# Picking expert 0's rows by f32r products of high and low parts instead of fp32 products

## The reference

```
h = tokens(x)                                  # patches @ W.T + b, a class token, positions
h = h + attn(layernorm(h))                     # causal sums, rank 64 factors, no softmax
xf = layernorm(h)                              # 1184 x 256
gates = softmax(xf @ w_router + b_router)      # 8 experts
topv, topi = top_k(gates, 2)
pos  = place of each choice in its expert's queue, in row order; keep = pos < cap   # cap = 185
buf[e, pos] = xf[row]                          # 8 experts x 185 rows x 256
out = gelu(buf @ w1 + b1) @ w2 + b2            # 256 -> 1024 -> 256 for each expert
h = h + sum over the two choices of weight * out[e, pos] / sum of kept weights
```

## Time and profile before

| | |
|---|---|
| median of 3 runs | 184.07 us (183.93 to 184.51) |
| the profiled execution | 182.03 us, of which its span is 180.2 us |
| PE busy | 160.3 us (89%) |
| DVE busy | 69.3 us (38%) |
| ACT busy | 62.5 us (35%) |
| POOL busy | 38.5 us (21%) |
[...]

### The profile page before, as it was taken

How to read it: one execution, slowest core, us unless ns; L and a number is a source line. 1 busy time by engine, 2 the same in 40 slices (tenths; PEclk the granted TensorE clock), 3 DMA queues, 4 the chain that set the end, 5 groups by cost and what they waited for, 6 DMA issues and landing times.

```text
span 180.2 us, 2947 instructions
## 1 busy us (share of the span) xinstructions
PE 160.3 (89%) x1065; PEld 151.3 (84%) x1065; DVE 69.3 (38%) x278; ACT 62.5 (35%) x151; POOL 38.5 (21%) x39
## 2 busy tenths in 40 slices
PE   1999999999999968898399999999999999999900
PEld 1679999997958967898399999999999999999800
DVE  0257567655787798968040110302003020020200
ACT  4306524424461157733005234061430604325010
POOL 1000000000000000007103708246171642306060
PEclk9999999999999999999969999999999999999995
DMA  6999900193005033604506777888777887401111
GB/s 198 423 418 419 349 0 0 18 362 133 0 0 155 2 91 89 192 21 114 204 0 230 182 224 188 282 242 238 212 152 272 241 259 245 66 0 22 20 22 20
DMA packets 17150, 28.41 MB, mean 158 GB/s; under 512 B 1273, under 2 KB 13635, under 8 KB 17013
## 3 DMA queue, kind: packets, MB, share of 16 engines
q1 hardware_dynamic: 14677, 25.42, 41.8%
q0 software_dynamic: 2464, 2.86, 9.0%
HBM read 24.14 MB, written 4.14 MB: 157 GB/s over the span
## 4 chain that ended last, share of the span: by engine, by line
PE 74%; DVE 12%; DMA 5%; POOL 2%; ACT 2%; issue 2%; POOLq 0%; ACTq 0%; DVEq 0%
PE ps L1094 22%; PE ps L1084 20%; PE ps L999 7%; PE ps L984 6%; PE ps L942 5%; DMA rows_in<-xrows,src_row 3%; PE ps L1031 3%; DVE bn L606 3%; PE ps L1014 2%; PE ps L1102 2%; DMA first_t<-first 2%; POOL out_rows L406 2%; PE ps L1072 1%; PE ps L1043 1%; DVE at_p L858 1%
## 5 line engine op out<-in xcount | busy, mean ns | idle before, releaser
L537 ACT ACTIVATE hid<-ps,b_cur 128x186 f32<-128x186 f32 x64 | 23.1, 412 | 62.2 <-PE ps L1084 62.2
L406 POOL DMA_INDIRECT out_rows<-out_s,dst_row x16 | 23.8, 1484 | 52.2 <-ACT out_s L548 43.8
L391 POOL DMA_INDIRECT rows_in<-xrows,src_row x14 | 13.9, 992 | 84.1 <-DVE src_row L809 80.1
L1094 PE MATMUL ps<-hid,w_even 128*128 128x186 f32 x128 | 23.4, 338 | 0.0
L831 DVE COPY buf_t<-ps 128x372 f32<-128x372 f32 (+1 forms) x8 | 4.2, 521 | 47.7 <-PE ps L1072 47.6
L1084 PE MATMUL ps<-buf_t,w_even 128*128 128x186 f32 x128 | 21.7, 321 | 0.6 <-DVE buf_t L831 0.6
L1094 PEld LDWEIGHTS ps<-hid,w_even 128*128 128x128 f32 x128 | 22.0, 202 | 0.0
L1084 PE MATMUL ps<-buf_t,patch_t 128*128 128x186 f32 x128 | 21.5, 320 | 0.0
L1094 PE MATMUL ps<-hid,patch_t 128*128 128x186 f32 x128 | 21.4, 321 | 0.0
L1084 PEld LDWEIGHTS ps<-buf_t,w_even 128*128 128x128 f32 x128 | 20.2, 190 | 0.8 <-issue 0.8
L1094 PEld LDWEIGHTS ps<-hid,patch_t 128*128 128x128 f32 x128 | 20.3, 189 | 0.0
(11 more groups left out here) (156 smaller groups left out, 222.3 us busy)
## 6 DMA issues: line engine op xcount, KB each, us to landing
w_even<-w SPq DMA_DIRECT2D x8, 1024.0 KB, 5.5
patch_t<-w SPq DMA_DIRECT2D x8, 1024.0 KB, 5.2
patch_t<-patches SPq DMA_DIRECT2D x2, 972.0 KB, 11.1
att<-attn SPq DMA_DIRECT2D x1, 1280.0 KB, 8.1
first_t<-first SPq DMA_DIRECT2D x1, 870.0 KB, 5.7
xrows<-xn SPq DMA_DIRECT2D x3, 288.0 KB, 2.4
out_rows<-h SPq DMA_DIRECT2D x3, 288.0 KB
first_t<-first SPq DMA_DIRECT2D x1, 580.0 KB, 4.0
```

Of the source, the lines that this page charges most:

```text
L391: pool.indirect_dma_start(out=rows_in[q][0:SIZES[s], s, :], out_offset=None, in_=xrows[:, :], in_offset=bass.IndirectOffsetOnAxis(ap=src_r ...
L406: pool.indirect_dma_start(out=out[:, :], out_offset=bass.IndirectOffsetOnAxis(ap=dst_row[0:SIZES[s], c:c + 1], axis=0), in_=out_s[q][0:SIZ ...
L537: ins = act.activation(hid[:, f, :], bank(pair)[:, (f % 2) * SL:(f % 2 + 1) * SL], ACT.Gelu, bias=b1_cur[q][:, f:f + 1])
L1094: ins = pe.matmul(bank(DOWN_BANKS[d])[:, 0:SL], w2_s[q][:, f, d * 128:(d + 1) * 128], hid[:, f, :], start=f == 0, stop=f == KF - 1)
```

## The change

ACT writes each normed tile a second time, as f32r, right after the group's `xn` (`rows_high`); for this it reads PSUM again. POOL subtracts it from `xn` (`rows_low`) and so makes the low part. The parts lie in the buffers of the patch stage. PE's `pick` waits for `rows_low` instead of for the norm's drain and multiplies high and low part in turn, as f32r. `onehot` becomes f32r. The copies to `h2` come behind the new ones; those of group C wait until group E is normed. ACT's Exp comes behind its copy of expert 0's half, and DVE's `take_in` of expert 0 comes ahead of `at_q` and of all of `at_p`, where it lay between two parts of `at_p`.

```diff
-        onehot = sb("onehot", [TT, NT, SL])
+        onehot = sb("onehot", [TT, NT, SL], f32r)
+        def normed(t, high):
+            held, rest = divmod(t, KP)
+            if high:
+                return (tok_h, tok_l)[held][:, rest]
+            return (patch_h, patch_l)[held][:, :, :].rearrange("p k n -> p (k n)")[:, rest * D:(rest + 1) * D]
...
             for g, (t0, n) in enumerate(GROUPS):
+                pool.wait_ge(rows_high, g + 1)
+                for t in range(t0, t0 + n):
+                    r = rows_of(t)
+                    ins = pool.tensor_tensor(normed(t, False)[0:r], xn[0:r, t], normed(t, True)[0:r], ALU.subtract)
+                ins.then_inc(rows_low, 1)
+
+            for g, (t0, n) in enumerate(GROUPS):
                 pool.wait_ge(rows_stored[g], 16 * (len(even_runs(TT)) + (t0 + n == NT) * len(even_runs(LAST))))
...
                     act.activation(xn[0:r, t], p[0:r, i * D:(i + 1) * D], ACT.Identity,
                                    bias=nmr[0:r, NT + t:NT + t + 1], scale=rstd[0:r, NT + t:NT + t + 1])
+                for i in range(n):
+                    t = t0 + i
+                    r = rows_of(t)
+                    ins = act.activation(normed(t, True)[0:r], p[0:r, i * D:(i + 1) * D], ACT.Identity,
+                                         bias=nmr[0:r, NT + t:NT + t + 1], scale=rstd[0:r, NT + t:NT + t + 1])
+                ins.then_inc(rows_high, 1)
+                if g != C:
+                    keep_rows(g)
+
+            def keep_rows(g):
+                if g == E:
+                    keep_rows(C)
+                p = slot(PLACE["norm2", g])
+                t0, n = GROUPS[g]
                 whole = n - (t0 + n == NT)
                 ins = copy(h2[:, t0:t0 + whole], p[0:TT, 0:whole * D].rearrange("p (t d) -> p t d", t=whole))
...
+            act.wait_ge(picked, 1)
+            copy(buf_t[0][:, 1:], pick_slot[:, 1:]).then_inc(half_ready, 1)
+
             act.wait_ge(below_ready, 1)
             act.activation(expd[:, :, :], below[:, :, :], ACT.Exp).then_inc(exp_ready, 1)
...
-            act.wait_ge(picked, 1)
-            copy(buf_t[0][:, 1:], pick_slot[:, 1:]).then_inc(half_ready, 1)
             for pair in range(PAIRS):
                 hidden(0, 0, pair)
...
             step(dve.tensor_tensor(slot_p[:, :, :], slot_p[:, :, :], lost[:, :, :], ALU.add))
+            take_in(0, 0, first=True)
             dve.tensor_tensor(at_q[:, :, :, :], grid(iota_slot[:, 0:SC], NT, 2, SC), spread(slot_q[:, :, :], NT, SC), ALU.is_equal)
...
-            find_slots(0, 3)
-            take_in(0, 0, first=True)
-            step(find_slots(3, NT))
+            step(find_slots(0, NT))
...
                         if t == first:
-                            drained(pe, "norm2", m)
+                            pe.wait_ge(rows_low, m + 1)
...
                     for k in range(KD):
-                        ins = pe.matmul(pick_slot[:, k, :], xn[0:r, t, k * 128:(k + 1) * 128],
-                                        onehot[0:r, t, :], start=t == 0, stop=t == NT - 1)
+                        for high in (True, False):
+                            ins = pe.matmul(pick_slot[:, k, :], normed(t, high)[0:r, k * 128:(k + 1) * 128],
+                                            onehot[0:r, t, :], start=high and t == 0, stop=not high and t == NT - 1)
```

More of the change, by code:

```diff
@@ L237, in vit_block @@
         patch_used = sem("patch_used")
+        rows_high, rows_low = sem("rows_high"), sem("rows_low")
         psum_filled = sem("psum_filled")
```

## The result

The changed kernel takes 193.27 us, the median of four runs (192.69 to 194.34), against 184.00 for the kernel before. The ratio is 1.056, with a 95% interval of 1.050 to 1.062. The sign was forecast; the time was forecast as 188.1 with a range to 190.4, so 5.2 us are missing from the forecast. The profiled execution took 194.34 us with a span of 192.5, and the mean granted clock of PE, as a share of its full speed, fell from 0.978 to 0.901. It is the longest of the four; the other three had a mean clock of 0.914 to 0.916. Some executions of a kernel are more than 1.5% longer than its fastest, and the ratios leave these out, so a ratio can differ from the quotient of two medians.

What follows compares the result with a forecast made beforehand. PE bounds the kernel from 90 us; the change moves that stretch's start, set by DVE's way to id_marks and the gather of expert 1. 1.47 + 0.62 + 1.63 + 0.1 + 0.2 = 4.0 us, giving 188.1, range 186.0 to 190.4.

Steps and rivals of the forecast that it cites:

- its term for the clock: Half clock around PE's wait for slots 2: 0.2 us added to the sum.
- the first stall: Norm of A: three high parts on ACT delay the copy that PE's transposes for E need, +1.47 us.
- The second: Norm of B: ACT's later copy delays PE's slots 1 and DVE behind it, +0.62 us.
- An f32r product of 186 columns: In pick: 0.112 us each, between 0.087 and 0.151, saving 44 x 0.048 us of PE's time.
- A subtraction on POOL: Making the low parts: 0.65 us a tile, between 0.31 and 0.73.
- The third stall: Last part of pick and take_in: DVE waits for PE, so id_marks start 1.63 us later.
- its upper bound for this stall: Last part of pick and take_in: +2.8 us with 0.73 on POOL and 0.151 on PE.
- its rival of 0.30 a product: In pick: f32r products cost twice 0.151, sum near 7, 191 us; chance 0.17 shared with the clock rival of 2.0 us.
- I take 0.1: POOL's subtractions for B beside DVE's onehot: 0.1 us, between nothing and 0.7 if fully hindered.
- a rival of 2.0 us: Clock falls during last pick and first half of up: sum 6.0, 190.1 us; chance 0.17 shared with slow products.
- the 2.1 us that shorter products save on PE: In pick: 44 shorter products save 2.1 us, but the first two parts end before waits, so only the last counts.
- The faster rival: Expert 1's gather ends before the w1 load, 3.1 less, and the clock holds, 1.76 less: 183.2 us; faster has chance 0.05.

Runs made afterwards that it cites:

- experiment 14: Changed kernel with 8, 6, 7, 5 and 9 spare products in PE's gaps before the end of pick and 11 in the gather's gap; 185.08 us, ratio 1.010.
- experiment 7: Kernel before plus POOL subtracting each tile of xn into unused buffers, with nobody waiting for it; 185.21 us, ratio 1.018.
- experiment 6: Changed kernel with DVE's take_in of expert 0 back in its old place between the parts of at_p; 191.84 us, ratio 1.052.
- experiment 13: Kernel before with f32r products in pick on wrong data, no high or low parts made or waited for; 186.84 us, ratio 1.019.
- experiment 3: Changed kernel with fp32 products in pick again; high and low parts still made and waited for, but not used; 189.14 us, ratio 1.033.
- experiment 4: Kernel before plus three more ACT writes of normed rows ahead of the h2 copy of group A alone; 186.41 us, ratio 1.020.
- experiment 11: Kernel before with 5 and 2 spare products around pick's second part and 11 in the gather's gap; 180.70 us, ratio 0.990.
- experiment 5: Kernel before plus 11 spare fp32 products in PE's wait for the gather of expert 1; 182.88 us over ten runs, ratio 0.990.
- experiment 1: Changed kernel with spare products, 3 to 6 in each place, in PE's five gaps before the look-up; 188.45 us, ratio 1.030.
- experiment 9: As experiment 8, but with the look-up back after the second quarter of up; 177.82 us, ratio 0.975 of the kernel before.
- experiment 8: Kernel before with ACT copying both halves, marks first, look-up after up's first quarter, w1 load of expert 2 behind the gather; 177.92 us, ratio 0.976.
- experiment 10: As experiment 8, but SP loads w1 of expert 2 early, without waiting for the gather; 177.73 us, ratio 0.975 of the kernel before.
- experiment 2: Changed kernel with high parts of groups A and B made from xn in SBUF behind the h2 copy; 192.25 us, ratio 1.049.

## Why the forecast was wrong

**What held.** The direct price is near what was added up. With the clock kept at 1.00 in both, up to the tail of their profiled executions, the kernels take 185.08 and 180.70: 4.4 us, or 3.8 by their ratios (1.0103 - 0.9897 of 184, within 1.6), where the sum without its term for the clock was 3.8. That it agrees so well is in part luck, since the terms that follow measure 1.4, 0.4, 2.6 and 0.5, 4.9 in all. Term by term: the first stall was put at 1.47 and is 1.37 (wait 1.81 against 0.44; three high parts take 1.37 on the chain). The second was put at 0.62 and is 0.44. An f32r product of 186 columns was put at 0.112 and is 0.11, which fits the reading by the weight load's duration (189 against 190 ns). A subtraction on POOL was put at 0.65; it takes 0.70 at groups A and B (2.10 for three) and 0.84 beside the `onehot` of C and E (4.21 for five). The third stall was put at 1.63 from `xn` of C to `id_marks`; in experiment 14 the way from `xn` of C to the look-up is 12.83 against 10.27, so 2.56, and the excess of 0.9 is POOL's pace: its five subtractions take 4.24 and not 5 x 0.65 = 3.25. Two sums of the forecast were off without effect: its upper bound for this stall (0.73 and 0.151) gives +2.6 and not +2.8, and its rival of 0.30 a product gives 7.6 us and 191.7, not 7 and 191.

**POOL beside DVE, mis-sized.** "I take 0.1" for group B's `onehot`: it went from 0.74 to 1.25, 0.5, near the upper bound that the forecast gave. Those of C and E went from 1.27 to 2.53. The forecast was right that DVE had time to spare there, but slowed POOL was on the path. Whether that needs two inputs from SBUF on both engines, as theory A of experiment 7 has it, no run separated; what the traces show is 0.74 and 1.25 for the same instruction.

**The clock, the step that failed.** The forecast had it as 0.2 us, the author's estimate without a row behind it, and as a rival of 2.0 us with part of a chance of 0.17. It cost 8.2 us in the changed kernel (193.27 against 185.08 when filled) and 3.3 in the kernel before (184.00 against 180.70), so 4.9 of the 9.3 us that the change costs. The ratios give 8.4 and 1.9, so 6.5 of 10.3. Three things in the working were wrong.

First, the forecast asked whether the clock would fall *on the path*, and held a fall elsewhere as free. At half clock PE did not stay off the path here. The last part of `pick`, 20 products, took 4.59 and the first half of `up` 5.30, and PE overtook DVE as the bound. So when experiment 6 takes DVE's wait in `take_in` out, PE still comes to the look-up after the marks: the stall was real (experiment 14, where PE waits 1.11 for the marks), and hidden under the clock.

Second, the 2.1 us that shorter products save on PE were counted as of no effect, since they end ahead of waits. Alone they cost 3.5 us (experiment 13), and with fp32 products in their place the changed kernel is 4 us faster (experiment 3). In experiment 13 the time taken from PE ahead of a wait was added to the wait (1.64 to 2.02), and the clock fell in it. The wait at A alone costs as much, 3.7 to 4.3 (experiment 4), of which 1.4 is its length. These shares are not a sum, since the parts set off the same falls.

Third, the evidence was there and was read past. The profiled execution of the kernel before took 182.03 and the median was 184.07, and the forecast carried those 2.0 us over as a constant. By the later executions of the same kernel they were the clock: those at a mean of 0.967 are 1.5 us longer than those at 0.978 (experiment 11), and the profiled one was at 0.978. Its row of 1.00 from 66 to 68 was taken as proof that the stretch bears gaps; in experiment 5, with the same wait of 1.64 there, the profiled execution was at 0.68 from 66 to 72. What keeps the clock up here is shown by experiments 1, 11 and 14: products in the gaps that compute nothing gave back 4.8, 3.3 and 8.2 us by the medians.

**What was hidden, and stayed so.** SP's stores (the last of `xn` issued by 83.23, the gather from 92.03 on), Exp with its two table loads (84.00 to 86.89), and the gather behaved as forecast: the gather took 5.48 and PE's wait for it was 3.36. The faster rival's mechanism, a gather that gets ahead of the `w1` load, is real (2.35 us instead of 5.55, experiment 9) and part of what experiments 8 to 10 gain, but the change does not set it off.

**Open.** How much of the half clock belongs to the wait at A, the shorter products and the wait for POOL each, when all three are there, was not separated. Nor is it known why the half clock behind the gather lasts 6.8 us in the changed kernel and 3.4 in the kernel before, when PE's wait is the same (3.36 and 3.41), or why one wait of 1.81 at A was followed by 6.8 us of it and another, in experiment 4, by 3.4.

## What to carry to other kernels

Before making PE's work shorter, ask what it waits for next: if PE isn't the bound there, the saving turns into idle time (1.64 became 2.02 in experiment 13), and idle time can take the clock from what follows, as it did here for 17 us. When a profile and the median differ by more than the runs' noise, compare the mean granted clock of the executions first; what the kernel before showed in one execution of eleven came in all six of experiment 13, once one of its gaps had grown. The cheap test is to fill PE's gaps with products that change nothing, and the better cure is to remove the wait: here it was enough to look the rows up a quarter of `up` earlier, with ACT making both copies, so that the gather was issued a microsecond ahead of the weight load (0.975, experiment 10).

## What the runs showed that was not expected

POOL and DVE slowed each other down by much: the same 111x186 compares took 1.27 us in the kernel before and 2.45 to 2.91 beside POOL's subtractions (experiments 7 and 14), and a subtraction 0.70 at group A and 0.84 beside them. The clock fell in or behind waits of only 1.2 to 2.0 us (1.17 in experiment 2, 1.81 at group A, 2.02 in experiment 13), and then stayed at half for up to 17 us although PE was busy for most of that time (4.00, 3.43 and 4.00 of each 4.00 us from 72 to 84 in experiment 13). The spare products around `pick` in experiment 11, where the clock was 1.00 up to 173 us, had zeros as one operand.
